# A mixture-of-experts stage rewritten as one program: deeper lag of the down products, splits on VectorE, routing weights through DRAM

## The chip, the cores and the metric

The kernel runs on one core of a Trainium2 chip. The metric is the device time in microseconds (us) of one execution. Three runs of the kernel before gave 3318.07, 3337.93 and 3340.95 us, median 3337.93. One more execution was profiled: 3319.7 us, of which 3317.8 us is the span from the first to the last instruction.

## The reference, cut to what matters

Two batches of 2048 tokens with 256 channels pass through a modulated attention layer and then through a modulated block of a second attention and a mixture of experts. All of it is float32. The change is about the last part:

```python
x = x + _attention(_rmsnorm(x, w_ln1), Wq, Wkva, Wkvb, Wo)     # only the product with Wo is in the changed stage
xn = _rmsnorm(x, w_ln2)
shared = jnp.mean(_experts(xf, sWg, sWu, sWd), axis=1)          # one shared expert
probs = jax.nn.softmax(xf @ Wgate + expert_bias, axis=-1)
topk_p, topk_i = jax.lax.top_k(probs, K)                        # K = 2 of E = 8
comb = jnp.sum(jax.nn.one_hot(topk_i, E) * (topk_p / jnp.sum(topk_p))[..., None], axis=1)
routed = jnp.einsum('ne,nec->nc', comb, _experts(xf, Wg, Wu, Wd))
out = residual + (shared + routed)
# _experts: g = silu(x @ Wg); u = x @ Wu; (g * u) @ Wd, per expert with I = 128 inner columns
```

The experts are computed densely: every token goes through all nine, and the routing weight of an expert, zero for most tokens, multiplies its inner activations.

## The kernel before, in words

The kernel is a row of stages, each in a `Block` with a barrier at its ends: modulation, first projections, first attention, second projections, second attention (`attention2`), and the experts' stage (`experts`, L1438). Matrix products are done three times on numbers split in two parts (`product3`, L127: low by high, high by low, high by high), so every operand exists as a rounded `_hi` and a rest `_lo = x - _hi`.

`experts` consists of three blocks, one after the other:

- `fold_weights` (L1396): GpSimd clears a tile, SyncE loads pieces of `Wkvb` and `Wo` and two constants, TensorE multiplies four pairs, ScalarE and VectorE split the products.
- `split_weights` (L134): ScalarE makes the high half of the experts' weights (L154), VectorE the low half (L160).
- the main block. Tokens are worked in eight blocks of 512 (four per batch; the two batches alternate). A token block has a *front* and nine *units*, one for each expert, the shared one last.

The front, by the step letters of the code: P splits the attention's output (load of 1 MB at L1545, high half on ScalarE L1593, low half on GpSimd L1571), A multiplies it by `Wo` (48 matmuls of 256 columns) and VectorE adds the residual; N and R are the norm (squares L1597, square root L1601); X transposes (L1765) and splits; L makes the logits (24 matmuls of 8 columns) and VectorE picks the two best; W takes the sigmoid of their difference; C transposes the weights.

A unit of expert j: G and U are the gate and up products (6 matmuls of 512 columns each) into the two halves of one of two PSUM pairs `pPair`; B (L1791) is one more matmul that spreads the routing weights of expert j over the 128 partitions; ScalarE takes the silu (L1616); VectorE multiplies it by the spread weights (L1718) and by the up product (L1726); ScalarE (L1620) and VectorE (L1642) split the result into `p_hi` and `p_lo`; D is the down product (12 matmuls of 256 columns), accumulated over the nine units in `pD`. After the last D, Y adds the residual on VectorE (L1734), and GpSimd multiplies by the modulation (L1574) and adds `x1` (L1578), before SyncE stores.

The order is written by hand and every engine runs through it (`order`, L1508). For each j it is G, B, U, then D of unit j-1, then a piece of the front of the *next* token block:

```python
after = {0: "P", 2: "A", 3: "NR", 4: "X", 5: "L", 6: "W", 7: "C"}
```

SyncE's own order (L1540 to L1557) for each block is: load of the attention's output for the next front, load of its residuals (one after the wait at L1551 for the output of the block before), then the wait for this block's result (L1555) and its store. The staging tiles of these loads and of the results lie in the memory of the unsplit weights (L1468, L1469).

Of the kernel before, what the change touches and what calls it, by code (L numbers as in the profile page):

```python
# [36 lines left out]

def modulation(nc, d, m):

    with ExitStack() as ctx:  # L40
        sb = lambda n, s, t=FP32: ctx.enter_context(nc.sbuf_tensor(n, s, t))
        sem = lambda n: nc.alloc_semaphore(n)
        cT, cE = sb("cT", [P, KT, B]), sb("cE", [P, KT, B])
# [11 lines left out]
        def _(sp):  # L55
# [4 lines left out]
            sp.dma_start(m.halves[:, :, :, :], d["halves"]).then_inc(loaded, 16)  # L60
# [31 lines left out]
        def _(dve):  # L92
# [11 lines left out]
            dve.tensor_copy(m.eye_half[:, :, :], m.halves[:, 0])  # L104
            dve.tensor_copy(m.after_half[:, :, :], m.halves[:, 1])
# [610 lines left out]
def attention2(nc, d, m):  # L716

    with ExitStack() as ctx:
# [35 lines left out]
        FILLS = 3  # L754
# [157 lines left out]
        def _(sp):  # L912
# [14 lines left out]
            for item in program:  # L927
# [23 lines left out]
        def _(pool):  # L951
            fills = [key1[b][ROWS:ROWS + 1].bitcast(FP32) for b in range(B)] + [ones[:, :]]
            for n, place in enumerate(fills):
                if n:
                    pool.wait_ge(filled, n)
                pool.memset(place, 1.0).then_inc(filled, 1)
# [481 lines left out]
def experts(nc, d, m):  # L1438

    with ExitStack() as ctx:  # L1442
        sb = lambda n, s, t=FP32: ctx.enter_context(nc.sbuf_tensor("e_" + n, s, t))
        sem = lambda n: nc.alloc_semaphore("e_" + n)
        sems = lambda n: [sem(f"{n}{b}") for b in range(2)]
        G, EX = HEADS // HG, E + 1
        wo_hi, wo_lo = sb("wo_hi", [P, G, C], F32R), sb("wo_lo", [P, G, C], F32R)
        wg_hi, wg_lo = sb("wg_hi", [P, KT, EX, I], F32R), sb("wg_lo", [P, KT, EX, I], F32R)
        wu_hi, wu_lo = sb("wu_hi", [P, KT, EX, I], F32R), sb("wu_lo", [P, KT, EX, I], F32R)
        wd_hi, wd_lo = sb("wd_hi", [P, EX, C], F32R), sb("wd_lo", [P, EX, C], F32R)  # L1450
        gate_hi, gate_lo = sb("gate_hi", [P, KT, E], F32R), sb("gate_lo", [P, KT, E], F32R)
        sel_st = sb("sel_st", [64, E, P])
        sel = sb("sel", [64, E, P], F32R)
        rank = sb("rank", [P, E])
        with ExitStack() as inner:
            st = lambda n, s, t=FP32: inner.enter_context(nc.sbuf_tensor("e_" + n, s, t))
            wo, kvb = st("wo", [P, G, C]), st("kvb", [P, G, P])
            fold_weights(nc, "e_fold", d, kvb,
                         [(wo[32 * j:32 * j + 32, :, :], d["Wo"].rearrange("(g j n) c -> j n g c", j=HG, n=HD2)[j, 0:32])
                          for j in range(HG)] + [(sel_st[:, :, :], d["sel"].rearrange("k (e p) -> k e p", e=E)),  # L1460
                                                 (rank[:, :], d["rank"].rearrange("(a n) -> a n", a=1).broadcast_to([P, E]))],
                         [(kvb[:, g, :], wo[:, g, :], wo_hi[:, g, :], wo_lo[:, g, :]) for g in range(G)])
        split_weights(nc, "e_w", [([], m.wg[:, :, :, :], wg_hi[:, :, :, :], wg_lo[:, :, :, :]),
                                  ([], m.wu[:, :, :, :], wu_hi[:, :, :, :], wu_lo[:, :, :, :]),
                                  ([], m.wd[:, :, :], wd_hi[:, :, :], wd_lo[:, :, :]),
                                  ([], m.gate[:, :, :], gate_hi[:, :, :], gate_lo[:, :, :])])

        o_st = m.wg[:, :, :, :].rearrange("p k e i -> p (k e i)")[:, 0:G * GT].rearrange("p (g t) -> p g t", g=G)  # L1468
        y = m.wu[:, :, :, :].rearrange("p k e i -> p (k e i)")[:, 0:B * NTILE * C].rearrange("p (b t c) -> p b t c", b=B, t=NTILE)  # L1469
        o_hi, o_lo = sb("o_hi", [P, G, GT], F32R), sb("o_lo", [P, G, GT], F32R)  # L1470
        xin, x1, x2 = sb("xin", [P, B, NTILE, C]), sb("x1", [P, B, NTILE, C]), sb("x2", [P, B, NTILE, C])
        xn, squares = sb("xn", [P, NTILE, C]), sb("squares", [P, NTILE, C])
        ssq, rms, rrms = sb("ssq", [P, NTILE]), sb("rms", [P, NTILE]), sb("rrms", [P, NTILE])
        xT_hi, xT_lo = sb("xT_hi", [P, B, KT, GT], F32R), sb("xT_lo", [P, B, KT, GT], F32R)
# [3 lines left out]
        comb = sb("comb", [P, NTILE, E])  # L1478
        combT = sb("combT", [64, B, GT], F32R)
# [4 lines left out]
        pB = ctx.enter_context(nc.psum_tensor("e_pB", [P, GT], FP32))  # L1484
        pG = ctx.enter_context(nc.psum_tensor("e_pG", [P, GT], FP32))

        filled, sel_ready, sp_passed = sem("filled"), sem("sel_ready"), sem("sp_passed")
        o_loaded, x_loaded, out_stored = sem("o_loaded"), sems("x_loaded"), sems("out_stored")
        x1_loaded, gate_psum = sems("x1_loaded"), sem("gate_psum")
        o_hi_ready, o_lo_ready = sem("o_hi_ready"), sem("o_lo_ready")  # L1490
        pair_psum, pair_read = sem("pair_psum"), sem("pair_read")
        x2_ready, ssq_ready, ms_ready, rms_ready, xn_ready = sem("x2_ready"), sem("ssq_ready"), sem("ms_ready"), sem("rms_ready"), sem("xn_ready")
        xT_hi_ready, xT_ready = sem("xT_hi_ready"), sem("xT_ready")
        g_psum, g_read, chain = sem("g_psum"), sem("g_read"), sem("chain")
        gap_ready, weight_ready, comb_ready, combT_hi_ready, combT_ready = (
            sem("gap_ready"), sem("weight_ready"), sem("comb_ready"), sem("combT_hi_ready"), sem("combT_ready"))
        b_psum, b_read = sem("b_psum"), sem("b_read")
        silu_ready, prod_ready, p_hi_ready, p_lo_ready = sem("silu_ready"), sem("prod_ready"), sem("p_hi_ready"), sem("p_lo_ready")
        down_done, y_sum, y_scaled, y_ready = sem("down_done"), sem("y_sum"), sem("y_scaled"), sem("y_ready")
        block = ctx.enter_context(nc.Block())  # L1500
        RING = 2

        FRONT = ("P", "A", "N", "R", "X", "L", "W", "C")

        def order(experts_too, front):  # L1508
            after = {0: "P", 2: "A", 3: "NR", 4: "X", 5: "L", 6: "W", 7: "C"}
            if not experts_too:  # L1510
                return [(s, 0) for s in FRONT]
            items = []
            for j in range(EX):
                items.append(("G", j))
                if j < E:
                    items.append(("B", j))
                items.append(("U", j))
                if j:
                    items.append(("D", j - 1))
                if front:  # L1520
                    items += [(s, 0) for s in after.get(j, "")]
            return items + [("D", E), ("Y", 0)]

        PAIRS = EX + 2

        def run(eng, work):

            work(order(False, True), -1, 1, 0, 0, 0, 0)
            for i in range(NGRP - 1):
                for b in range(B):  # L1530
                    work(order(True, True), i, b, i + b, 1 - b, 2 + PAIRS * (2 * i + b), b)
# [365 lines left out]
```

## Time and profile before

| What | us |
|---|---|
| Median of three runs | 3337.93 |
| Profiled execution, its own time | 3319.7 |
| Its span | 3317.8 |
| First instruction of the experts' stage (GpSimd's clearing, L1406) | 2727.9 |
| Start of the first load of the main block | 2751.1 |
| Start of the first unit's matmuls | 2791.5 |
| End of the last down product | 3307.5 |

The experts' stage is the last 590 us of the span. Everything before 2727.9 us is other stages, which the change touches in the second attention's list of loads and in one GpSimd fill alone. In the 40 slices of the page one slice is 82.9 us, so the stage is the last seven and a bit.

### The profile page before, as it was taken

What the parts mean: (1) busy time and instruction counts of PE and PEld (TensorE: products, weight loads), DVE (VectorE), ACT (ScalarE), POOL (GpSimd) and SP (SyncE); (2) the same over time, 40 slices, a digit from 0 to 9 for tenths busy, and PEclk for the clock granted to TensorE, in tenths of its full rate; (3) what the DMA queues carried; (4) which work ended last, traced back from release to release, by engine and by line L of the source; (5) the groups of instructions that cost most, each with busy time, mean ns of one, the idle gap of its engine ahead of it and who ended that gap; (6) DMA issues with size and microseconds to landing.
All of it is one profiled execution on the core that took longest, in us unless ns stands there. A gap on an engine that the chain in (4) does not pass through costs nothing. (4 is left out here: it accounts for less than half of the span.)

```text
span 3317.8 us, 47823 instructions
## 1 busy us (share of the span) xinstructions
PE 2852.9 (86%) x18768; PEld 1797.9 (54%) x18768; DVE 2049.9 (62%) x3301; ACT 1543.2 (47%) x3161; POOL 1312.8 (40%) x402
## 2 busy tenths in 40 slices
PE   3659999999999457668999999999999965888888
PEld 2534444444444145545566666666666634666666
DVE  4647888788885156647676776767676503444444
ACT  1225777677777222214455555555555533332232
POOL 3410000000000054525879788887979771111111
PEclk8967999899999578878999999999999977999889
DMA  3660331233300356571151321213131001101100
GB/s 94 202 124 5 44 45 19 31 44 46 39 10 8 101 166 183 188 184 30 23 129 42 68 49 45 54 37 68 23 68 42 11 17 51 32 32 61 35 32 13
DMA packets 153665, 207.01 MB, mean 62 GB/s; under 512 B 47840, under 2 KB 88928, under 8 KB 150304
## 3 DMA queue, kind: packets, MB, share of 16 engines
q1 hardware_dynamic: 152336, 198.58, 25.5%
q10 hardware_dynamic: 1104, 5.38, 0.5%
q8 instruction: 148, 2.42, 0.3%
q14 instruction: 77, 0.63, 0.1%
HBM read 121.59 MB, written 81.79 MB: 61 GB/s over the span
## 5 line engine op out<-in xcount | busy, mean ns | idle before, releaser
L990 ACT ACTIVATE a_prob<-a_pS 128x512 f32<-128x512 f32 (+3 forms) x1280 | 630.4, 534 | 594.8 <-PE a_pS L1072 269.2
L971 POOL TENSOR_TENSOR a_zsum<-a_zsum,a_prob 128x2048 f32<-128x2048 f32 (+1 forms) x200 | 882.0, 4410 | 50.9 <-ACT a_prob L990 24.2
L629 DVE TENSOR_REDUCE a_rowmax<-a_pR 128x2 f32<-128x1024 f32 (+3 forms) x640 | 651.7, 1061 | 144.1 <-PE a_pR L668 90.8
L610 ACT ACTIVATE a_prob<-a_pS 128x512 f32<-128x512 f32 (+3 forms) x1280 | 591.6, 539 | 287.6 <-PE a_pS L690 183.3
L1009 DVE TENSOR_REDUCE a_rowmax<-a_pR 128x2 f32<-128x1024 f32 x384 | 462.3, 1223 | 133.0 <-PE a_pR L1054 129.3
L1071 PE MATMUL a_pS<-a_q,a_key 128*128 128x512 f32 (+3 forms) x1280 | 507.9, 397 | 30.1 <-ACT a_prob L990 24.1
L1072 PE MATMUL a_pS<-a_q,a_key 65*128 65x512 f32 (+3 forms) x1280 | 474.7, 371 | 0.0
L1054 PE MATMUL a_pR<-a_key,a_q 128*128 128x512 f32 (+3 forms) x1280 | 395.8, 392 | 34.7 <-DMA a_q<-mid_q 22.4
L690 PE MATMUL a_pS<-a_q,a_key 49*128 49x512 f32 (+3 forms) x1280 | 406.7, 452 | 21.0 <-DMA a_q<-a_neg 15.7
L668 PE MATMUL a_pR<-a_key,a_q 48*128 48x512 f32 (+3 forms) x1280 | 330.3, 453 | 22.5 <-DMA a_q<-mid_qk 16.3
L1071 PEld LDWEIGHTS a_pS<-a_q,a_key 128*128 128x128 f32 x1280 | 247.8, 194 | 161.2 <-ACT a_prob L990 72.4
L706 PE MATMUL a_pO<-a_prob,a_val 128*32 128x512 f32 (+3 forms) x2560 | 317.0, 569 | 0.2
L1012 DVE CUSTOM_DVE_ANT_0 a_pR<-a_pR,causal 128x384 f32<-128x384 f32 (+3 forms) x512 | 240.5, 513 | 105.0 <-PE a_pR L1054 103.2
L690 PEld LDWEIGHTS a_pS<-a_q,a_key 49*128 49x128 f32 x1280 | 193.4, 197 | 185.6 <-ACT a_prob L610 115.3
L595 POOL COPY a_val<-v 128x256 f32<-128x256 f32 x32 | 11.4, 400 | 713.1 <-PE a_pO L706 698.6
L1054 PEld LDWEIGHTS a_pR<-a_key,a_q 128*128 128x128 f32 x1280 | 227.9, 198 | 86.3 <-issue 32.1
L1084 PE MATMUL a_pO<-a_prob,lat 128*32 128x512 f32 (+3 forms) x2560 | 262.5, 536 | 0.4 <-ACT a_prob L990 0.4
L1072 PEld LDWEIGHTS a_pS<-a_q,a_key 65*128 65x128 f32 x1280 | 246.2, 192 | 28.9
L668 PEld LDWEIGHTS a_pR<-a_key,a_q 48*128 48x128 f32 x1280 | 157.5, 198 | 163.1 <-DVE a_rowmax L629 96.1
L1026 DVE RECIPROCAL a_pR<-a_pR 128x512 f32<-128x512 f32 x32 | 107.7, 3366 | 129.7 <-PE a_pR L1095 129.7
L969 POOL TENSOR_TENSOR a_zsum<-a_prob 128x2048 f32<-128x2048 f32 x24 | 110.3, 4596 | 178.7 <-ACT a_prob L990 178.7
L1574 POOL TENSOR_TENSOR wu<-wu,mod 128x1024 f32<-128x1024 f32 x8 | 19.1, 2389 | 386.9 <-DVE wu L1734 386.9
(237 smaller groups left out, 4094.1 us busy)
## 6 DMA issues: line engine op xcount, KB each, us to landing
a_q<-mid_q SPq DMA_DIRECT2D x192, 256.0 KB, 6.4
a_key<-mid_qk SPq DMA_DIRECT2D x42, 256.0 KB, 9.0
a_q<-mid_qk SPq DMA_DIRECT2D x42, 256.0 KB, 15.8
mid_qk<-p_qk_hi SPq DMA_DIRECT2D x32, 256.0 KB, 2.8
mid_qk<-p_qk_lo SPq DMA_DIRECT2D x32, 256.0 KB, 3.3
mid_q<-p_n_hi SPq DMA_DIRECT2D x32, 256.0 KB, 3.0
mid_q<-p_n_lo SPq DMA_DIRECT2D x32, 256.0 KB, 3.3
mid_q<-p_r_hi SPq DMA_DIRECT2D x32, 256.0 KB, 2.4
```

The costliest lines, as they stand in the source:

```text
L610: act.activation(prob[:, n % 4, h, at:GT], pS[:, (HG * n + h) % NS, at:GT], ACT.Exp).then_inc(exp_ready, 1)
L629: dve.tensor_reduce(rowmax[:, c % 2, :, j, t, kc], pR[:, bank, :, 0:n], axis=AX.X, op=ALU.max).then_inc(r_read, 1)
L668: mm = pe.matmul(pR[:, bank, half, 0:n], q[g % 2][rows48, j, at:at + P], key[g % 2][rows48, j, GT * kc:GT * kc + n], start=True, stop=kc < c)
L690: mm = pe.matmul(pS[:, n % NS, at:GT], key[g % 2][rows49, h // 2, P * kt:P * kt + P], q[g % 2][rows49, h // 2, c * GT + at:(c + 1) * GT], ...
L706: mm = pe.matmul(pO[32 * h:32 * h + 32, at:GT], val[g % 2][:, kt, h, :], prob[:, n % 4, h, at:GT], start=(kt == 0), stop=kt == 4 * c + 3)
L971: pool.tensor_tensor(zsum[:, ring, :, at:GT], zsum[:, ring, :, at:GT], prob[:, step % 4, :, at:GT], ALU.add).then_inc(z_added, 1)
L990: act.activation(prob[:, n % 4, h, at:GT], pS[:, (HG * n + h) % NS, at:GT], ACT.Exp, scale=SCALE).then_inc(exp_ready, 1)
L1009: dve.tensor_reduce(rowmax[:, c % 2, 2 * j:2 * j + 2, t, kc], pR[:, bank, :, :], axis=AX.X, op=ALU.max).then_inc(r_read, 1)
L1054: mm = pe.matmul(pR[:, bank, half, 0:n], q0[:, c, 2 * j + half, P * t:P * t + P], key0[b][:, GT * kc:GT * kc + n], start=True, stop=True)
L1071: pe.matmul(pS[:, n % NS, at:GT], key0[b][:, keys], q0[:, c, h, at:GT], start=True, stop=False)
L1072: mm = pe.matmul(pS[:, n % NS, at:GT], key1[b][0:ROWS + 1, keys], q1[0:ROWS + 1, c, h, at:GT], start=False, stop=not diagonal)
L1084: mm = pe.matmul(pO[32 * h:32 * h + 32, at:GT], m.lat[:, b * (T // P) + kt, :], prob[:, n % 4, h, at:GT], start=(kt == 0), stop=kt == 4 * ...
```

## The change

- The three blocks of the experts' stage become one: the folding and the weight splits are steps of one program, between the steps of the first front. Their loads (`e_kvb`, `wo`, `rank`) move into the second attention's list of loads, nine more DMAs there, behind a wait for four GpSimd fills.
- The program runs over all 72 units (0 to 8 of each token block, the shared expert now first), batch by batch. D of a unit stands behind the products of the unit after the next. The front of the next block is spread one step per unit, A behind unit 0 of a block, and the split of the attention's output ("O") behind unit 8, two blocks ahead. Its load is issued at step X.
- The matmul B and its operands are gone. The routing weights, transposed, are stored to DRAM (16 KB) and loaded back by one source row for all 128 partitions: 6 experts (1536 KB) at once after the store, 2 (512 KB) later. The silu is multiplied by that tile.
- GpSimd does nothing in the stage. The low half of the attention's output and both operations of Y are on VectorE, Y in three parts behind units 1, 2 and 3 of the next block.

```diff
 def attention2(nc, d, m):
                     load_keys(sp, 1, slice(0, T), key_loaded[1])
+                    sp.wait_ge(filled, FILLS)
                     for src, place in m.expert_loads:
                         sp.dma_start(place, src).then_inc(experts_loaded, 16)
...
+            m.expert_loads = [(heads_kvb[j], m.e_kvb[32 * j:32 * j + 32, :, 32 * j:32 * j + 32]) for j in range(HG)]
+            m.expert_loads += [(heads_wo[j, 0:32], m.wo[32 * j:32 * j + 32, :, :]) for j in range(HG)]
+            m.expert_loads += [(d["rank"].rearrange("(a n) -> a n", a=1).broadcast_to([P, E]), m.rank[:, :])]
 def experts(nc, d, m):
-            fold_weights(nc, "e_fold", d, kvb,
...
-        split_weights(nc, "e_w", [([], m.wg[:, :, :, :], wg_hi[:, :, :, :], wg_lo[:, :, :, :]),
...
-        def order(experts_too, front):
-            after = {0: "P", 2: "A", 3: "NR", 4: "X", 5: "L", 6: "W", 7: "C"}
...
+        def order():
+            items = [("fold", 0), ("O", 0), ("split", 0), ("split", 1), ("A", 0), ("N", 0), ("split", 2), ("R", 0), ("X", 0),
+                     ("split", 3), ("L", 0), ("K", 0), ("O", 1), ("W", 0), ("C", 0)]
+            for n in range(BLOCKS):
+                front = {0: [("A", n + 1)], 1: [("N", n + 1)], 2: [("R", n + 1)], 3: [("X", n + 1)], 4: [("L", n + 1)],
+                         5: [("K", n + 1)], 6: [("W", n + 1)], 7: [("C", n + 1)], 8: [("O", n + 2)]}
+                for j in range(UNITS):
+                    k = UNITS * n + j
+                    items.append(("U", k))
+                    items += [x for x in front[j] if x[1] < BLOCKS]
+                    if k >= 2:
+                        items.append(("D", k - 2))
+                    if n and j < 4:
+                        items += [("Y", n - 1, j - 1)] if j else []
+            last = UNITS * BLOCKS
+            return items + [("P", last), ("D", last - 2), ("D", last - 1)] + [("Y", BLOCKS - 1, part) for part in range(3)]
 # SyncE
+            def load_spread(n, part):
+                experts_in = slice(0, EARLY) if part == 0 else slice(EARLY, E)          # EARLY = 6
+                if n:
+                    sp.wait_ge(prod_ready, UNITS * (n - 1) + experts_in.stop + 1)
+                sp.dma_start(spread[:, experts_in], d["comb"][n, experts_in].rearrange("(a e) t -> a e t", a=1)
+                             .broadcast_to([P, experts_in.stop - experts_in.start, GT])).then_inc(spread_loaded[part], 16)
...
+                if step == "C":
+                    s = n % 2
+                    sp.wait_ge(combT_ready, n + 1)
+                    sp.dma_start(d["comb"][n], combT[:, s, :]).then_inc(comb_stored[s], 16)
+                    sp.wait_ge(comb_stored[s], 16 * (n // 2 + 1))
+                    load_spread(n, 0)
+                if step == "U" and n % UNITS == 1:
+                    load_spread(n // UNITS, 1)
+                if step == "X" and n + 1 < BLOCKS:
+                    load_o(n + 1)                    # waits for the matmuls of A of block n
 # ScalarE, step U
+                    act.activation(silu[:, n % 2, :], pPair[:, pairs["U", n] % 2, 0, :], ACT.Silu).then_inc(silu_ready, 1)
+                if step in "UP" and n:
+                    high_half(n - 1)
 # VectorE
+                if step == "O":
+                    dve.wait_ge(o_hi_ready, n + 1)
+                    dve.tensor_tensor(o_lo[:, :, :], o_lo[:, :, :].bitcast(FP32), o_hi[:, :, :], ALU.subtract).then_inc(o_lo_ready, 1)
...
+                if step == "U":
+                    dve.wait_ge(silu_ready, n + 1)
+                    if j:
+                        dve.tensor_tensor(prod[:, s, :], silu[:, s, :], spread[:, j - 1, :], ALU.mult).then_inc(prod_begun, 1)
+                    if n:
+                        low_half(n - 1)
+                    dve.wait_ge(pair_psum, use + 1)
+                    dve.tensor_tensor(prod[:, s, :], pPair[:, use % 2, 1, :], (prod if j else silu)[:, s, :], ALU.mult).then_inc(prod_ready, 1)
...
+                    if part == 1:
+                        dve.tensor_tensor(y, y, m.mod[:, n // NGRP, 5, :].unsqueeze(1).broadcast_to([P, NTILE, C]), ALU.mult).then_inc(y_scaled, 1)
+                    if part == 2:
+                        dve.wait_ge(x1_loaded, 16 * (n + 1))
+                        dve.tensor_tensor(y, y, x1[:, :, :], ALU.add).then_inc(y_ready, 1)
 # TensorE
-                    if step == "B":
-                        pe.matmul(pB[:, :], sel[:, j, :], combT[:, b, :], start=True, stop=True).then_inc(b_psum, 1)
+                    if use >= 2:
+                        pe.wait_ge(pair_read, use - 1)     # of steps U, A and X
+                if step == "L":
+                    if n == 0:
+                        pe.wait_ge(split_lo, len(splits))
+                if step == "D":
+                    if j == 0 and at:
+                        pe.wait_ge(y_sum, at)
+                    pe.wait_ge(p_lo_ready, n + 1)
```

## Rows read from the trace of the kernel before

**Rows 1.** The page: the span.
```profile
span 3317.8 us, 47823 instructions
```

**Rows 2.** Windows: length; busy us (instructions) of PE, PEld, DVE, ACT, POOL; PEclk; DMA.
```profile
2727.90:2751.10 23.20, 3.90 (x8) 2.17 (x8) 9.28 (x8) 7.79 (x8) 0.53 (x1) 0.57 0.16 38
...
2751.10:2791.50 40.40, 15.90 (x85) 15.01 (x86) 7.02 (x26) 8.91 (x16) 5.44 (x2) 0.58 0.31 104
...
2791.50:2851.30 59.80, 56.72 (x316) 44.87 (x314) 28.80 (x55) 23.52 (x38) 4.62 (x1) 0.98 0.00 1
...
2919.20:2988.10 68.90, 58.27 (x309) 46.41 (x308) 29.20 (x54) 21.64 (x36) 9.33 (x3) 0.90 0.12 39
...
3055.90:3126.70 70.80, 61.29 (x310) 48.92 (x309) 29.30 (x54) 21.63 (x36) 9.35 (x4) 0.86 0.12 38
...
3264.60:3307.50 42.90, 41.97 (x219) 32.87 (x218) 19.03 (x26) 11.03 (x18) 4.77 (x2) 1.00 0.04 13
...
3307.50:3317.80 10.30, 0.04 (x1) 0.00 (x0) 1.22 (x1) 0.00 (x0) 4.67 (x2) 0.60 0.15 51
```

**Rows 3.** Timeline of TensorE, third block: start, us, what [idle before, releaser].
```profile
2935.33 0.79 PE L1791 MATMUL e_pB<-e_combT,e_sel 64*128 64x512 f32 x1 [7.47 <-DVE e_prod L1718]
```

**Rows 4.** Timeline of ScalarE, same stretch.
```profile
2932.16 1.91 ACT L1593 ACTIVATE e_o_hi<-wg 128x2048 fp32r<-128x2048 f32 x1 [9.39 <-DMA wg<-mid_o]
```

**Rows 5.** Chain of work that ended last, same stretch: start, us, what.
```profile
2924.68 7.46 DMA wg<-mid_o
```

**Rows 6.** Windows of TensorE's two clock levels; columns as in Rows 2.
```profile
2930.80:2941.00 10.20, 5.37 (x15) 3.83 (x16) 5.20 (x5) 3.92 (x5) 4.53 (x1) 0.50 0.23 74
...
3104.90:3111.60 6.70, 6.70 (x17) 4.74 (x18) 3.72 (x16) 0.60 (x1) 0.00 (x0) 0.50 0.00 0
...
3217.50:3307.00 89.50, 85.44 (x479) 68.47 (x479) 41.57 (x75) 27.93 (x48) 4.79 (x2) 1.00 0.02 7
```

**Rows 7.** Timeline of TensorE, fifth block: the first matmul of L.
```profile
3102.60 0.17 PE L129 MATMUL e_pG<-e_gate_hi,e_xT_lo 128*128 128x8 f32 x1
```

**Rows 8.** Timeline of TensorE, last block: L129 opens each group of matmuls.
```profile
3295.83 0.39 PE L129 MATMUL e_pPair<-e_xT_hi,e_wg_lo 128*128 128x512 f32 x1
...
3299.24 0.28 PE L129 MATMUL e_pD<-e_wd_hi,e_p_lo 128*128 128x256 f32 x1
...
3300.66 0.39 PE L129 MATMUL e_pPair<-e_xT_hi,e_wg_lo 128*128 128x512 f32 x1
...
3303.41 0.29 PE L129 MATMUL e_pD<-e_wd_hi,e_p_lo 128*128 128x256 f32 x1
```

**Rows 9.** Windows of one tile, TensorE: e_wo_hi (A), e_xn (X), e_pG (L, C).
```profile
3217.50:3264.60 47.10, 5.92 (x32) 1.00 0.01 1
...
3217.50:3264.60 47.10, 1.04 (x8) 1.00 0.01 1
...
3217.50:3264.60 47.10, 3.33 (x28) 1.00 0.01 1
```

**Rows 10.** Groups by line from 2650 us: busy, mean ns, idle before, releasers.
```profile
L1571 POOL TENSOR_TENSOR e_o_lo<-wg,e_o_hi 128x2048 fp32r<-128x2048 f32 x8 | 36.3, 4538 | 99.5 <-ACT e_o_hi L1593 99.5
...
L154 ACT ACTIVATE e_wu_hi<-wu 128x2304 fp32r<-128x2304 f32 x1 | 2.1, 2106 | 0.0
...
L160 DVE TENSOR_TENSOR e_wg_lo<-wg,e_wg_hi 128x2304 fp32r<-128x2304 f32 x1 | 2.6, 2557 | 2.5 <-ACT e_wg_hi L154 2.5
```

**Rows 11.** Timeline of VectorE, third block.
```profile
2936.70 2.53 DVE L1642 TENSOR_TENSOR e_p_lo<-e_prod,e_p_hi 128x512 fp32r<-128x512 f32 x1 [0.70 <-ACT e_p_hi L1620]
```

**Rows 12.** DMA issues: KB each, median us to landing.
```profile
mid_o<-a_out SPq DMA_DIRECT2D x32, 128.0 KB, 2.0
...
wmod<-in_wmod_dram SPq DMA_DIRECT2D x1, 1536.0 KB, 6.3
```

**Rows 13.** Chain of waits, first front: ScalarE's table load before the square root.
```profile
2773.76 1.28 ACT L1601
```

**Rows 14.** Timeline of SyncE's queue, folding: four DMA issues.
```profile
2730.29 1.86 SPq L1415 DMA_DIRECT2D e_wo<-in_Wo_dram  x4
```

More of the change, by code:

```diff
@@ L1451, in experts @@
[L1451 to L1457, printed above, removed]
-            fold_weights(nc, "e_fold", d, kvb,
[L1459 to L1462, printed above, removed]
@@ L1524, in experts @@
[L1524 to L1531, printed above, removed]
-            i = NGRP - 1
-            work(order(True, True), i, 0, i, 1, 2 + PAIRS * 2 * i, 0)
-            work(order(True, False), i, 1, 0, 0, 2 + PAIRS * (2 * i + 1), 1)
-        tok = lambda name, b, i: d[name].rearrange("b (i t p) c -> b i p t c", t=NTILE, p=P)[b, bass.ds(i, 1)].rearrange("a p t c -> (a p) t c")
+        splits = [(m.wg[:, :, :, :], wg_hi[:, :, :, :], wg_lo[:, :, :, :]), (m.gate[:, :, :], gate_hi[:, :, :], gate_lo[:, :, :]),
+                  (m.wu[:, :, :, :], wu_hi[:, :, :, :], wu_lo[:, :, :, :]), (m.wd[:, :, :], wd_hi[:, :, :], wd_lo[:, :, :])]
@@ new lines, in _ @@
+            load_o(0)
+            load_xin(0)
+            load_xin(1)
+            load_x1(0)
+            for step, n, *rest in program:
+                if step == "C":
[8 more added lines that the diff above has]
+                    load_o(n + 1)
+                if step == "L" and n + 1 < BLOCKS and n:
+                    load_xin(n + 1)
+                if step == "Y" and rest[0] == 2:
+                    sp.wait_ge(y_ready, n + 1)
+                    sp.dma_start(token_block(d, "out", *divmod(n, NGRP)), x2[:, n % SLOTS]).then_inc(out_stored[n % SLOTS], 16)
+                    if n + 1 < BLOCKS:
+                        load_x1(n + 1)
@@ new lines, in _, with link, low_half @@
+            per_token = lambda t: t.unsqueeze(2).broadcast_to([P, NTILE, E])
+            ranks = m.rank[:, :].unsqueeze(1).broadcast_to([P, NTILE, E])
+            links = 0
+            def link(ins):
+                nonlocal links
+                links += 1
+                ins.then_inc(chain, 1)
+                dve.wait_ge(chain, links)
+            def low_half(k):
+                dve.wait_ge(p_hi_ready, k + 1)
+                dve.tensor_tensor(p_lo[:, k % 2, :], prod[:, k % 2, :], p_hi[:, k % 2, :], ALU.subtract).then_inc(p_lo_ready, 1)
@@ L1802, in _ @@
-            run(pe, work)
+                if step == "D":
+                    at, j = divmod(n, UNITS)
+                    if j == 0 and at:
+                        pe.wait_ge(y_sum, at)
+                    pe.wait_ge(p_lo_ready, n + 1)
+                    for t in range(NTILE):
+                        tokens = slice(P * t, P * t + P)
+                        mm = product3(pe, pD[:, t, :], p_hi[:, n % 2, tokens], p_lo[:, n % 2, tokens], wd_hi[:, expert(j), :], wd_lo[:, expert(j), :],
+                                      j == 0 and t % 2 == 0, j == UNITS - 1, skip_group_check=True)
+                    mm.then_inc(down_done, 1)
```

513 lines of the change are left out of this document (223 added, 290 removed).

## The prediction

> **What bounds the kernel now.** I started at the page, for the span [rows 1], and cut the experts' stage into stretches by the windows view [rows 2]. It takes 590 us: 23.2 us for folding and splitting, 40.4 us for the first front, then eight token blocks, and 10.3 us behind the last down product. A middle block takes 68.9 us with TensorE busy for 58.3; VectorE (29.2), ScalarE (21.6) and GpSimd (9.3) are not near it. So TensorE's queue sets the time, and three things make a block longer than its products need.
>
> - It waits. 68.9 - 58.3 = 10.6 us of the block it is idle, 7.47 of them in one gap [rows 3]. There ScalarE, in order, stands for 9.39 us in front of the split of the attention's output, for a load [rows 4]. The chain of waits says why the load is late: its 7.46 us begin only after SyncE's queue has stored the block before, for which it waits on GpSimd's last addition (L1578) [rows 5].
> - Its clock falls. Behind such a gap it is granted half of full speed (1.2 instead of 2.4 GHz) for 10.2 us [rows 6]. Over the block the share is 0.90, so 0.10 x 68.9 x 2 = 13.8 us at half speed and 6.9 us lost.
> - Products that the change drops: B, eight times per block.
>
> The last block has no front and runs nearly without gaps: 42.9 us at a clock of 1.00, 42.0 busy [rows 2]. It shows what units cost when nothing is late.
>
> **One unit after the change.** In that block a unit with B repeats after 3300.66 - 3295.83 = 4.83 us; in the shared unit, which has no B, gate and up take 3303.41 - 3300.66 = 2.75 us; a down product takes 3300.66 - 3299.24 = 1.42 us [rows 8]. A unit without B is 2.75 + 1.42 = 4.17 us. The bound above is that removing B saves only its own time of some 0.4 us (4.83 - 4.17 is 0.66): 0.24 x 64 = 15 us more. I take 4.17, as the row is that very sequence.
>
> **The front on TensorE.** A 5.92, X 1.04, L and C 3.33 us busy [rows 9], 10.3 in sum. Modelled ends overlap the next matmul by 0.16 to 0.2 us, once per piece, so 9.6.
>
> **Blocks.** 72 x 4.17 + 7 x 9.6 = 300.2 + 67.2 = 367.4 us, if nothing is late. Is something late? I follow each queue, from TensorE's first matmul of a unit as zero.
>
> - *Unit.* Gate ends at 1.4; silu to 2.0; VectorE's product with the spread tile to 2.7, the low half of the unit before to 3.4, the product with up to 4.1 (instructions of 512 columns take some 0.7, 19.03 / 26 [rows 2]). The pair must be free at 8.3 (two units) and the low half is wanted at 6.9, since D lags by two units. Now D stands one unit behind and waits. Moving it costs nothing.
> - *O behind unit 8.* ScalarE 2.7 to 4.6; VectorE, 2048 columns by the row of 2304 [rows 10], 2.27 us, to 6.9. A behind the next unit 0 starts at 4.17 + 2.75 = 6.9. No slack: the cover is the down product and the unit's products, and each 1 us beyond costs 1 us.
> - *X, L, K, W, Y on VectorE.* Its work per block becomes 29.2 + 2.3 + 2 x 1.22 = 33.9 of 47.1 us. The first part of Y (1.22 us [rows 2]) has the 2.75 us of unit 2 as cover before D of the next block needs `pD`. GpSimd's own instructions go, and with them what VectorE loses beside them: a low half of 2.53 us next to GpSimd's subtraction [rows 11] instead of 0.7.
> - *ScalarE* keeps its table loads and stays at 22 us.
> - *The routing weights.* From C to the silu of unit 1 of the next block TensorE has 2 D, unit 8, unit 0, A, D and a gate product: 3 x 1.42 + 2 x 2.75 + 5.8 + 1.4 + silu 0.6 = 17.5 us. Against it: copy 0.6, store of 16 KB 2.0 (nearest row 128 KB), load of 1536 KB 6.3 (a load from as many different rows) [rows 12], 8.9 in sum. Hidden with 8.6 us over, and 4 more before TensorE runs dry. In the first block the cover is some 12 us, still enough. The 512 KB behind it are due five units later. SyncE waits for the store before it loads, with nothing urgent behind it.
> - *Loads of the attention's output* are issued at X, four units ahead: the 7.47 us gap goes.
>
> A rule of the Trainium skill speaks against that load (DMA: Bandwidth & Descriptors, Latency and other measured facts): copies whose 128 rows lay megabytes apart by a power of two ran at 103 instead of 207 GB/s, put down to all streams meeting one memory channel. One row read by all 128 would be that case. By it the load takes 15.3 us and the sum grows by 2 to 3 us in the first block alone.
>
> **Clock.** With the gaps gone their falls should go too. But one fall has no gap in front: at 3104.9 TensorE is busy for all of 6.7 us at half speed, just behind the start of L's matmuls of 8 columns at 3102.60 [rows 6, 7]. The two blocks with a share of 0.86 (one in [rows 2]) have such a fall, the other five have not. L stays. I take two falls again, 2 x 6.7 / 2 = 6.7 us, bounds 0 and seven (23.5). The first unit starts after idling: in the first block now 0.02 x 59.8 us of share are missing [rows 2], +1.2. For small waits 0.3 per front, +2.1.
>
> The skill's page TensorE: Matmul & The Clock Gate (HAM oscillation) lets the clock fall for an idle engine only. By it there are no such falls and the sum is 6.7 us lower; the row contradicts it.
>
> **Prologue.** Now the 23.2 us pass before the load of the first front, then 40.4 us to the first unit [rows 2]. After, the load starts at +0.6 and the fold lies beside it (5 us of load; four small products 4 us). On the path: 0.6 + 40.4, less GpSimd's 4.54 for VectorE's 2.27 = -2.3; the third split before R, 2.11 + 2.56 less the 1.28 us table load that it hides [rows 13], +3.4; the fourth before L, its ScalarE half beside VectorE's work on X, +3.3; O of block 1 before W, +2.3 [rows 10]. Sum 47.7 instead of 63.6 us: 15.9 saved, first unit at 2775.6. Bounds: all splits hidden (38.7) and none of ScalarE's (54).
>
> **Second attention.** Nine more DMA issues at one place; at 1.86 / 4 = 0.47 us each [rows 14] they hold SyncE's queue for 4.2 us. TensorE has work from other loads there; I take 0, bounds 0 and 4.2.
>
> **Tail.** 10.3 us now, with VectorE 1.22 and GpSimd 4.67 [rows 2]; three VectorE parts 3.66 instead of 5.89: 8.1.
>
> **Sum.** 2775.6 + 367.4 + 6.7 + 1.2 + 2.1 + 8.1 = 3161.1 us of span, and 1.9 around it (3319.7 against 3317.8): 3163 against 3319.7, 157 us less. The profiled run lies 18 us under the median of the three runs, which spread over 23 us; so from 3337.9: **3181 us**. By its own bounds this case reaches from 3163 to 3205.
>
> **Rivals.**
>
> *The clock does not hold.* If blocks still miss a tenth, each loses 6.9 us as now: 48 instead of 6.7, 3222 us. For it: falls without a gap. Against: 89.5 us at 1.00 in the densest stretch, with one L in it [rows 6]. Chance 0.15.
>
> *VectorE's order becomes the wait.* It does nearly everything in line and waits for ScalarE and TensorE between. If TensorE keeps the 10.6 - 7.5 = 3.1 us of other idle time per block, at A for O or at D for Y, and each costs 5.1 us of clock: 7 x 8.2 = 57, 3238 us. Against: the slack of the units. Chance 0.13.
>
> *The load is no earlier in effect*, since SyncE holds it behind stores and loads of the routing weights. Gap and clock stay, 7 x 12.6 = 88: 3269 us. Against: what stands before it is due earlier. Chance 0.03.
>
> *The broadcast load is slow* (the side on which it is slower than before). The tile is single; its load cannot start before C and unit 6's product, so a block repeats in no less than load time + 2.6 + 30 us. Up to 19 us nothing happens. From 34 us on (five times the 6.3) it is as slow as before; at 45 us a block takes 78, 8 x 30 = 241 more: 3422 us. For it: no row shows a load of this size from one row. Against: the row of a plain load. Chance 0.05. The skill's rule above is a mild form of it and changes nothing but the first block.
>
> Better than my case, with no falls and splits hidden: 0.06. My case: 0.58.
>
> **Numbers.** 3181 us. Under 3150 lies 0.06, over 3245 the last two rivals and part of the third, so 3150 to 3245 holds a good 8 in 10. What can be told from no change is about 1%, 33 us. Faster by more: all but part of the slow load, 0.93; within 1% 0.02; slower 0.05.
>
> **What would show it.** First unit near 2776; windows of 47 us per block with TensorE over 95% busy and a clock of 0.97 or more; no gap over 1 us at A; VectorE never waiting for the tile of routing weights from the second block on; that load landing in 6 to 9 us. I am wrong if VectorE's product waits for the load, if the clock's share stays at 0.9 with TensorE busy, or if A waits for the low half.

## The result, and the profile after

| | before | after |
|---|---|---|
| Median of 4 runs each, us | 3332.82 | 3157.15 (3152.57 to 3171.17) |
| Ratio | | 0.9485, 95% interval 0.9438 to 0.9532 |
| Span of the profiled run | 3317.8 | 3150.7 |
| Experts' stage | 589.9 | 428.4 |
| of it until the first gate product | 63.2 | 46.8 |
| from the first gate product to the last down product | 516.4 | 373.8 |
| behind it | 10.3 | 7.9 |

The kernel is 5.1% faster. The prediction was 3181 us, 3150 to 3245. The time lies in that range, and the mechanism of the main case came true. But it lies 6 us under the 3163 to 3205 that the prediction gave as this case's own bounds; the point on the sum, below, says which term did that. (The 63.6 us of the prediction until the first unit are 63.2 by the first gate product itself, at 2791.17.)

The page, the span, against [rows 1]:
```profile
span 3150.7 us, 47527 instructions
```
Windows of the changed kernel, columns as in [rows 2]: prologue, a middle block, a block just behind a clock fall, the whole stretch of the units, the tail.
```profile
2722.30:2769.07 46.77, 20.09 (x93) 17.93 (x93) 20.33 (x33) 16.82 (x21) 0.00 (x0) 0.57 0.24 79
2821.10:2868.70 47.60, 47.60 (x303) 42.51 (x302) 29.28 (x56) 20.86 (x36) 0.00 (x0) 1.00 0.30 100
2894.36:2943.25 48.89, 48.89 (x307) 43.53 (x307) 29.27 (x56) 20.86 (x36) 0.00 (x0) 1.00 0.28 96
2769.07:3142.80 373.73, 373.65 (x2318) 332.77 (x2316) 219.46 (x417) 156.22 (x271) 0.00 (x0) 0.99 0.27 91
3142.80:3150.70 7.90, 0.03 (x1) 0.00 (x0) 3.67 (x3) 0.00 (x0) 0.00 (x0) 0.76 0.20 66
```
A middle block takes 47.6 us instead of 68.9, and TensorE is busy for all of it, at full clock. Over 373.7 us it is idle for 0.1.

What TensorE waits for in the stage (us in total, times, longest of one; in front of the arrow what waits, behind it what ended the wait). All five stand before the first unit:
```profile
PE e_pPair L1746 <- DVE e_xn L1653: 9.4, 1, 9.4
PE e_pPair L1725 <- PEq L1839: 7.6, 1, 7.6
PE e_pG L129 <- DVE e_wd_lo L1634: 6.0, 1, 6.0
PE e_pPair L129 <- DVE e_o_lo L1637: 5.7, 1, 5.7
PE e_pG L1765 <- DVE e_comb L1687: 5.7, 1, 5.7
```
The gap of [rows 3] and ScalarE's wait of [rows 4] have no counterpart: ScalarE's main wait is now for TensorE.

Timeline of VectorE where a block ends, then of TensorE; against the prediction's "no slack" at O:
```profile
2862.78 2.29 DVE L1637 TENSOR_TENSOR e_o_lo<-e_o_lo,e_o_hi 128x2048 fp32r<-128x2048 f32 x1 [0.43 <-ACT e_o_hi L1578]
```
```profile
2865.22 0.36 PE L129 MATMUL e_pPair<-e_wo_hi,e_o_lo 128*128 128x256 f32 x1
```
The low half ends at 2865.07, A begins at 2865.22: 0.15 us to spare.

DMA issues of the page, against [rows 12]:
```profile
e_spread<-mid_comb SPq DMA_DIRECT2D x8, 1536.0 KB, 6.3
```
One source row per expert, read for all 128 partitions, lands in 6.3 us, as fast as the load of this size from different rows.

The one clock fall among the units; timeline of TensorE at the end of an L, and the window of the fall:
```profile
2888.66 0.17 PE L129 MATMUL e_pG<-e_gate_hi,e_xT_lo 128*128 128x8 f32 x1
...
2890.81 0.25 PE L131 MATMUL e_pG<-e_gate_hi,e_xT_hi 128*128 128x8 f32 x1
2890.92 0.34 PE L129 MATMUL e_pG<-e_gate_hi,e_xT_lo 128*128 128x8 f32 x1
```
```profile
2890.95:2894.36 3.41, 3.41 (x17) 3.41 (x18) 1.33 (x7) 0.00 (x0) 0.00 (x0) 0.50 0.91 262
```
There is no gap in front of it, and the small matmuls of L stretch from 0.25 to 0.34 us. The fall costs half its 3.41 us.

**Where 142.6 us of the units' stretch went.** I split the stretch of each run into three parts. The first is TensorE's idle time. The second is half of what it was busy at half clock (lost clock). The rest is its products at full clock, with what small waits take from their overlap. All come from its matmuls and the clock changes in the trace.

| run | stretch | idle | lost clock | products |
|---|---|---|---|---|
| before | 516.4 | 63.5 | 33.5 | 419.3 |
| after | 373.8 | 0.1 | 2.9 | 370.8 |
| after, second profile | 376.9 | 0.1 | 6.1 | 370.7 |
| e1_early_load | 454.4 | 21.2 | 11.8 | 421.4 |
| e2_lag_two | 501.8 | 62.5 | 24.9 | 414.4 |
| e3_early_and_lag | 433.1 | 11.3 | 4.9 | 416.9 |
| a1_lag_one | 432.0 | 43.6 | 4.4 | 384.0 |
| a2_dummy_b | 411.9 | 0.1 | 7.4 | 404.5 |
| a3_late_tile | 410.2 | 17.8 | 19.3 | 373.1 |
| a4_later_tile | 453.3 | 49.7 | 33.5 | 370.1 |
| a5_y_gpsimd | 405.1 | 17.3 | 16.4 | 371.3 |
| a6_o_gpsimd | 399.0 | 13.1 | 15.2 | 370.7 |
| a7_prologue | 379.2 | 0.1 | 8.8 | 370.3 |
| a8_spread_l | 374.5 | 0.1 | 1.3 | 373.1 |

Of the 142.6 us, 63.4 were idle time, 30.6 lost clock and 48.5 products.

**Where the clock falls.** In these profiles every fall that begins among the units begins at one of two places. One is a wait of TensorE of 1.8 us or more (all shorter ones are under 1 us): during it, or up to 1.5 us behind its end. The other is the lot of 24 small matmuls of L: 2.1 to 4.1 us behind its first matmul. Counted are the waits, and those with a fall; the lots (seven in each run, a8 has none in one piece), and those with a fall; and the clock lost at each.

| run | waits of 1.8 us or more, each | with a fall | lost there | lots of L with a fall | lost there |
|---|---|---|---|---|---|
| before | 7 of 1.8, 6 of 6.2 to 7.5 | 11 of 13 | 25.1 | 2 | 6.8 |
| e1_early_load | 7 of 1.8 | 3 of 7 | 5.1 | 2 | 5.1 |
| e2_lag_two | 6 of 8.1 to 8.9 | 6 of 6 | 16.5 | 4 | 6.8 |
| e3_early_and_lag | none | | | 2 | 3.4 |
| after / its second profile | none | | | 1 / 2 | 1.7 / 5.1 |
| a1_lag_one | 7 of 2.6 | 2 of 7 | 3.2 | 0 | 0 |
| a2_dummy_b | none | | | 3 | 5.1 |
| a3_late_tile | 7 of 1.8 to 2.2, 1 of 3.0 | 3 of 8 | 5.1 | 6 | 11.9 |
| a4_later_tile | 8 of 5.9 to 6.5 | 8 of 8 | 20.4 | 7 | 11.9 |
| a5_y_gpsimd | 6 of 2.8 | 6 of 6 | 10.0 | 3 | 5.1 |
| a6_o_gpsimd | 6 of 2.2 | 1 of 6 | 1.7 | 6 | 11.9 |
| a7_prologue | none | | | 3 | 6.8 |

What is missing to the lost clock above is the slow start of the first unit (1.0 to 2.3 us). In all, 41 of 91 lots have a fall.

### The profile page after: what moved, and what is told of

Same layout as the page of the kernel before. It is cut to its first block and busy times, and to the rows that moved or that the text cites. A ratio compares the mean times of both kernels' runs of the same rounds, so it can differ in the third digit from the quotient of the medians.

```text
span 3150.7 us, 47527 instructions
## 1 busy us (share of the span) xinstructions
PE 2765.7 (88%) x18704; PEld 1769.9 (56%) x18704; DVE 2053.7 (65%) x3314; ACT 1534.5 (49%) x3157; POOL 1237.4 (39%) x377
## 5 line engine op out<-in xcount | busy, mean ns | idle before, releaser
L672 PE MATMUL a_pR<-a_key,a_q 48*128 48x512 f32 (+3 forms) x1280 | 330.3, 453 | 22.8 <-DMA a_q<-mid_qk 16.6
L1089 PEld LDWEIGHTS a_pO<-a_prob,lat 128*32 128x32 f32 x2560 | 71.6, 109 | 123.3 <-issue 88.2
```

The costliest lines, as they stand in the source:

```text
L672: mm = pe.matmul(pR[:, bank, half, 0:n], q[g % 2][rows48, j, at:at + P], key[g % 2][rows48, j, GT * kc:GT * kc + n], start=True, stop=kc < c)
L1089: mm = pe.matmul(pO[32 * h:32 * h + 32, at:GT], m.lat[:, b * (T // P) + kt, :], prob[:, n % 4, h, at:GT], start=(kt == 0), stop=kt == 4 * ...
```

## Experiments

Ratios are to the kernel before on the same chip, with 95% intervals.

**From the kernel before: one part alone.**

*e1_early_load.*
```diff
 SyncE: load of the attention's output for the next front
-    behind the wait for this block's result, the store, and the residuals' wait
+    ahead of them; the rest of the order as it is
```


> The kernel before with one thing changed: SyncE issues the load of the next attention output ahead of the wait for the block's result, so it has landed when ScalarE comes to it. Theory (the gap and what the clock does behind it are worth what the trace shows): the 7.2 us gap and 10.2 us at half clock (5.1 us lost) go in seven blocks: 7 x 12.3 = 86 us less, ratio 0.974, stage (first instruction to end) 504 instead of 590 us. Rival (another wait takes its place, since ScalarE, GpSimd and VectorE still have the same work in line): only the gap or less, under 50 us, ratio 0.985 or above.

Measured: 0.979 (0.974 to 0.985), stretch -62.0. Between the theory and its rival. The theory had read two sizes wrongly. The kernel before has this wait in six blocks, not seven:
```profile
PE e_pB L1791 <- DVE e_prod L1718: 41.2, 6, 7.5
```
And of the 58.0 us of falls behind these six gaps TensorE is busy for 33.3 only, so 16.6 us are lost, not 7 x 5.1. The theory should have said 41.2 + 16.6 = 57.8 us, which fits the 62.0. Waits of TensorE for the low half in e1, from 2770 us on:
```profile
PE e_pD L129 <- DVE e_p_lo L1649: 20.6, 22, 1.8
```
The 7.5 us gap is gone with 42.3 us of idle time and 21.7 of lost clock. What stays is the down product one unit behind, beside GpSimd's long subtraction.

*e2_lag_two.*
```diff
-                    items.append(("D", j - 1))
+                    items.append(("D", j - 2))       # and ("D", E - 1), ("D", E) at the end of a block
```


> The kernel before with the down products two units behind instead of one, nothing else. Theory: the waits of down products for the low half (1.8 + 0.3 + 0.7 us per block) and one fall of the clock (3.4 us, 1.7 lost) go: 7 x 4.5 = 31 us less, ratio 0.991. Rival (the late load sets the block, and what is gained before it is waited for there): about nothing, ratio 0.997 to 1.0.

Measured: 0.995 (0.992 to 0.998), stretch -14.6, half of what the theory said.
```profile
PE e_pB L1791 <- DVE e_prod L1718: 51.2, 6, 8.9
PE e_pPair L1765 <- DVE e_xn L1661: 10.2, 8, 6.0
PE e_pPair L129 <- DVEq L1728: 6.1, 7, 0.9
```
(The 6.0 us at X are the first front's.) The waits of D are gone, but the big gap grew from 7.5 to up to 8.9 us: TensorE only comes sooner to the product that stands for the load. Idle time fell by 1.0 us in all.

*e3_early_and_lag*: both edits.

> Both at once on the kernel before. Theory (TensorE's queue is then dense at full clock, and the two add): 86 + 31 = 117 us less, ratio 0.965, stage 473 us; what is left to the changed kernel's 428 is the matmul B (64 x 0.66 = 42) and the prologue (16). Rival (not additive: one cures the other's wait): 86 us, ratio 0.974.

Measured: 0.977 (0.973 to 0.982), stretch -83.3, 7 more than the two alone (76.6). The lag is worth 21.3 us once the load is early. In total time it comes no lower than its rival's figure, and the medians of e1 and e3 lie 5.7 us apart where the stretches differ by 21.3. In e3's profile the experts' stage begins 16 us later; such differences come between profiles of one code too (below), so the total time can't settle it. Against the changed kernel 59.3 us are left, 46.1 of them products.

**From the changed kernel: one part taken back.**

*a1_lag_one.*
```diff
-                    if k >= 2:
-                        items.append(("D", k - 2))
+                    if k >= 1:
+                        items.append(("D", k - 1))
```


> The changed kernel with the down products one unit behind. Theory: VectorE makes the low half only behind the product with the tile of the next unit, 3.5 us after the unit's first matmul, the down product is due at 2.75: TensorE waits 0.75 us in each of 72 units, 54 us more, stage 482 instead of 428, ratio 0.965. Rival (the lag is not needed, VectorE has slack): under 10 us more, ratio 0.95.

Measured: 0.971 (0.966 to 0.977), stretch +58.2. Waits of TensorE in the stage:
```profile
PE e_pD L129 <- DVE e_p_lo L1625: 25.4, 45, 0.7
PE e_pD L129 <- DVE e_x L1711: 18.2, 7, 2.6
```
The size is the theory's, a part of its content is not: 18.2 us are Y's first addition, which frees `pD` and with a lag of one has no unit to hide behind. Another 13.2 us are no gaps at all but products that lose their overlap behind 45 short waits (384.0 against 370.8). Nothing of it is clock (+1.5).

*a2_dummy_b*: adds, in 56 units, a matmul of B's shape that nobody reads.
```diff
+                        if half == 0 and j < 7:
+                            if j == 0:
+                                pe.wait_ge(combT_ready, at + 1)
+                            pe.matmul(pG[:, 1, :], wg_hi[0:64, 0, 0, :], xT_hi[0:64, at % 2, 0, :], start=True, stop=True)
```


> The changed kernel with one more matmul of B's shape (64 rows, 512 columns) between the gate and the up product in units 0 to 6 of each block, 56 in all; nobody reads its result. Theory (removing B saves the difference of a unit with and without it, 4.83 - 4.17): 56 x 0.66 = 37 us more, stage 465. Rival (only its own 0.42 us): 23.5 us more, stage 452.

Measured: 0.964 (0.959 to 0.969), stretch +38.1, of which products +33.7: 33.7 / 56 = **0.60 us** each, though the matmul itself is shown with less:
```profile
L1779 PE MATMUL e_pG<-e_xT_hi,e_wg_hi 64*128 64x512 f32 x56 | 28.4, 507 | 0.0
```
So leaving out B is worth 0.60 a unit, 38.5 us in 64 units, near the 0.66 of [rows 8] and not the 0.42 of the bound. The other 10 of 48.5 us of products have no shown cause. Some may be of the kind that a1 shows, overlap lost behind short waits; but e3, whose down products hardly wait for the low half any more (0.7 us in all), still has 7.6 of them (416.9 - 370.8 - 38.5).

*a3_late_tile* and *a4_later_tile*: the tile of routing weights is loaded later, behind A in unit 0 and behind unit 1's products.
```diff
-                    load_spread(n, 0)                # at step C
+                if step == "U" and n % UNITS == 0:   # a4: == 1
+                    sp.wait_ge(pair_psum, ...)       # a3: the matmuls of A of the next block; a4: those of unit 1
+                    load_spread(n // UNITS, 0)
```


> The changed kernel with the load of the routing weights (1536 KB) issued only behind A, some 3.4 us before VectorE wants it; it lands 3.1 us late. Theory (TensorE has 4 us more before it runs dry; only the first part of Y, queued behind on VectorE, is 1.5 us late for the next block's first down product): 7 x 1.5 = 10 us more. Rival A (each us that VectorE waits is a us of time): 8 x 3.1 = 25 us more. Rival B (hidden): 0.

> The same load issued behind the products of unit 1, 2.8 us later still. Theory: the first part of Y is 5.7 us late, TensorE stands for that long in seven blocks, and its clock falls behind it as it did behind the 7 us gap (3.4 to 5.1 us lost): 7 x 9.1 to 10.8 = 64 to 75 us more, clock share of the stage 0.9. Rival (the gap alone, since it is shorter and the clock holds): 40 us more, share 0.98.

Measured: a3 0.962 (0.952 to 0.973), stretch +36.4; a4 0.975 (0.972 to 0.979), +79.5. Waits of VectorE and TensorE in a3:
```profile
DVE e_prod L1697 <- DMA e_spread<-mid_comb: 47.3, 8, 6.2
```
```profile
PE e_pD L129 <- DVE e_x L1713: 14.5, 7, 2.2
PE e_pD L129 <- DVE e_p_lo L1627: 3.0, 1, 3.0
```
VectorE stands some 6 us in each block and TensorE only about 2: the cushion of the lag is there, and what breaks through is again Y's first addition, but for the first block's 3.0 us. I had expected the tile 3.1 us late and Y 1.5; it is 5.9 and 2.1. The price is double TensorE's idle time, since 16.4 us of clock come with it. Timeline of TensorE and window of the fall behind a gap, second block:
```profile
2835.66 0.38 PE L129 MATMUL e_pD<-e_wd_hi,e_p_lo 128*128 128x256 f32 x1 [1.91 <-DVE e_x L1713]
```
```profile
2837.15:2840.56 3.41, 3.41 (x10) 2.69 (x9) 2.88 (x8) 2.06 (x4) 0.00 (x0) 0.50 0.00 0
```
Only three of the eight gaps have such a fall. The other six falls, with 11.9 us of the clock lost, come 12 to 15 us behind the gap, at L. First matmul of L in the fourth block, and the window of the fall:
```profile
2949.70 0.17 PE L129 MATMUL e_pG<-e_gate_hi,e_xT_lo 128*128 128x8 f32 x1
```
```profile
2953.20:2956.61 3.41, 3.41 (x13) 2.93 (x12) 0.70 (x4) 0.00 (x0) 0.00 (x0) 0.50 0.81 257
```
The late tile brings them (six of seven lots here, one or two of seven in the changed kernel). How a gap that is over by then does it stays open, and in a1 gaps of 2.6 us brought none at L.

+17.7 idle, +16.4 lost clock, +2.3 products. I had reckoned 10 us, without clock. In a4, with gaps up to 6.5 us, it is +49.6 and +30.6, in sum a little over the theory's 64 to 75 us; there all eight gaps and all seven lots have a fall, and its rival failed. Even so a4 is faster than the kernel before.

*a5_y_gpsimd* and *a6_o_gpsimd*: Y's multiplication and last addition, or O's low half, back on GpSimd.
```diff
-        dve.tensor_tensor(y, y, m.mod[...], ALU.mult)       # and the addition of x1; a6: o_lo = o_lo - o_hi
+        pool.tensor_tensor(y, y, m.mod[...], ALU.mult)      # likewise, same waits and semaphores
```


> The changed kernel with the multiplication and the last addition of Y back on GpSimd. Theory (off the path but for the tail): 2.3 us more. Rival (VectorE's instructions with two operands in SBUF are held up beside GpSimd's, 2.5 us instead of 0.7 as in the kernel before, and A or D then waits): 10 us or more.

> The changed kernel with the low half of the attention's output back on GpSimd. Theory (no slack there: VectorE's ends 0.15 us before A starts; GpSimd takes 4.54 instead of 2.29 us): 2.1 us of wait in seven blocks and 2.3 in the prologue, 17 us more; with VectorE held up beside it up to 30. Rival (hidden behind the products): 2.3 us more.

Measured: a5 0.966 (0.957 to 0.974), stretch +31.3; a6 0.957 (0.951 to 0.963), +25.2. Timelines of GpSimd, VectorE and TensorE in a5:
```profile
2843.55 2.41 POOL L1619 TENSOR_TENSOR e_x<-e_x,mod 128x1024 f32<-128x1024 f32 x1 [119.61 <-DVE e_x L1725]
2846.04 2.73 POOL L1623 TENSOR_TENSOR e_x<-e_x 128x1024 f32<-128x1024 f32 x1
```
```profile
2844.27 2.24 DVE L1709 TENSOR_TENSOR e_prod<-e_silu,e_spread 128x512 f32<-128x512 f32 x1 [0.80 <-ACT e_silu L1607]
2846.44 2.89 DVE L1639 TENSOR_TENSOR e_p_lo<-e_prod,e_p_hi 128x512 fp32r<-128x512 f32 x1
...
2850.73 1.14 DVE L1667 TENSOR_SCALAR e_xn<-e_x,e_rrms 128x256 f32<-128x256 f32 x4
```
```profile
2852.02 0.52 PE L1753 MATMUL e_pPair<-eye,e_xn 128*128 128x128 f32 x3 [2.84 <-DVE e_xn L1667]
```
The rival was right. VectorE is relieved of 2.44 us and loses more: two instructions of 0.69 us take 2.24 and 2.89 while GpSimd works, each ending some 0.55 us behind GpSimd's. The norm starts 8.48 us behind Y's first addition (2842.25) instead of 4.72, X comes 2.84 us late in six blocks, 17.0 us, and the clock adds 13.5, 10.0 of it at these waits. The tail is 2.3 us longer, as the theory had it. In a6 A waits for the slower low half, 2.2 us in six blocks, 13.0 us, and the clock adds 12.3: a fall at one wait of six, the rest at L. The 2.3 us more in the prologue did not come (46.4 us for 46.8).

**The changed kernel, improved.**

*a7_prologue.*
```diff
-            items = [..., ("split", 1), ("A", 0), ("N", 0), ("split", 2), ("R", 0), ("X", 0),
-                     ("split", 3), ("L", 0), ("K", 0), ("O", 1), ("W", 0), ("C", 0)]
+            items = [..., ("split", 1), ("split", 2), ("split", 3), ("A", 0), ("N", 0), ("R", 0), ("X", 0),
+                     ("O", 1), ("L", 0), ("K", 0), ("W", 0), ("C", 0)]
```


> The changed kernel with all four weight splits before A of the first front and the split of block 1's attention output before its logits, so that they run while TensorE does A and L. Theory: 3.4 + 3.3 + 2.3 = 9.0 us less on the way to the first unit, 38.1 instead of 47.1 us, ratio to the kernel before 0.946. Rival (VectorE is still splitting when A ends, or squares wait on ScalarE): 3 us or less.

Measured: 0.951 (0.946 to 0.956). The first unit comes 38.6 us behind the fold's first matmul instead of 46.8, as expected; but the units of this profile have three clock falls, 13.7 us together, where the first profile of the changed kernel has one of 3.4 us: +5.4. (The expectation of a8 counts four, with the slow start of the first unit.) The total time doesn't show the gain.

*a8_spread_l*: a7, and L in four lots.
```diff
+                        if half == 0 and j == 4 and at + 1 < BLOCKS:   # behind the gate half of unit 4
+                            route(at + 1, 0)                           # 6 of the 24 matmuls
...                                                                     # lot 1 behind U, 2 within the down product, 3 behind it
```


> The changed kernel with two edits: the prologue of the run a7 (all four splits before the first attention product, the second o load's halves before the routing's) and the 24 routing logit products of a block laid in four lots of 6: behind the gate half of U in the fifth unit, behind U, in the middle of the down product and behind it, in place of one lot of 24. Work is the same. Theory: TensorE's clock falls within the stage begin in the lot of 24 (after: one, 2.9 us lost; a7: four, 6 us lost); with the lot broken up, none is left, the first-G-to-last-D loop takes 373.8 - 2.9 = 371 us, the prologue stays at 38 to 39 us against 46.8, and the stage is 11 us shorter than the changed kernel's: ratio to before 0.9485 - 0.0033 = 0.945, and 0.9965 of the changed kernel beside it. Rival: the falls come from the mean of what TensorE did before, not from that lot, and then they stay: loop 375 to 380 us with as many falls as in a7, ratio within 0.1% of a7's beside it. Second rival: the logits are done 1.4 us later and VectorE, which waits for them in its order, comes late for the next unit: TensorE idles about 1 us at the down product in each of 7 blocks, +7 us.

> The changed kernel itself once more, beside a8 on the same chip, so that a8's gain is read against it and not against the kernel before. Theory: 0.9485 of the kernel before within its interval, stage 425 to 435 us, loop 371 to 380 us by how many clock falls of some 3 us each it meets (one in the first profile). Rival: the first profile was a lucky one, and the loop has as many falls as a7's (four or more), 379 us or above.

Measured: a8 0.9485 (0.9447 to 0.9523), the changed kernel beside it 0.9512 (0.9476 to 0.9548), with a stage of 431.3 and a stretch of 376.9 us, as its theory had it. Windows of a8: prologue, units, tail.
```profile
2729.67:2766.99 37.32, 19.02 (x93) 16.89 (x93) 20.41 (x33) 16.84 (x21) 0.00 (x0) 0.59 0.29 99
2766.99:3141.45 374.46, 374.37 (x2318) 331.06 (x2316) 219.38 (x417) 156.30 (x271) 0.00 (x0) 1.00 0.27 91
3141.45:3149.30 7.85, 0.00 (x0) 0.00 (x0) 3.67 (x3) 0.00 (x0) 0.00 (x0) 0.73 0.19 67
```
In a8 the clock holds from 2769.61 to 3145.08. The two falls of the changed kernel's second profile:
```profile
2964.29:2971.12 6.83, 6.83 (x26) 6.15 (x26) 1.33 (x7) 0.47 (x1) 0.00 (x0) 0.50 0.59 181
3015.49:3018.91 3.42, 3.42 (x16) 3.32 (x16) 1.33 (x7) 0.00 (x0) 0.00 (x0) 0.50 0.90 276
```
Their L's begin at 2962.14 and 3012.87. In the four profiles without gaps (two of the changed kernel, a7, a2), nine falls come at the 28 lots of 24, each 2.2 to 4.1 us behind the lot's first matmul and nowhere else in blocks of some 48 to 53 us. That they come at L is shown by this. In a8 there is none in 7 blocks. If 9 in 28 were the plain chance, none in 7 would come one time in 15, so that breaking L up cures them is likely but not proven.

Cutting L up costs 2.5 us of products (373.1 against a mean of 370.6 in the changed kernel and a7), over half of the 4.6 us that the clock gives back (1.3 lost against a mean of 5.9). The gain of a8 is the prologue: the stage takes 419.6 us against 428.4 and 431.3. Mean of six runs each, 3156.2 against 3166.3 us: 10.2 less, 95% interval 0.4 to 20.0. That is the best version here, by 0.3%, just told apart from the changed kernel. Of its rivals, the second failed, as TensorE waits for nothing among a8's units; the first, that the falls don't hang on the lot, found no fall to rest on.

## Why the prediction was right, point by point

- **Bound and mechanism.** Idle time, lost clock, and B: all three went. The measured block of 47.6 us is 9 x 4.17 + 9.6 = 47.1 and 0.5 of small change. The present cost of the clock was misread, though. The prediction took half of all time at half clock, 6.9 us a block, for lost; but in 10.2 us of [rows 6] TensorE is busy for 5.37 only, and only busy time loses by the clock. The trace of before has 33.5 us of lost clock in all, 4.8 a block, and the big gap in six blocks, not seven. So the 5.1 us of clock a block in the second and third rival are too much (the gap and the clock behind it are 57.8 us in e1's terms, where the third has 88). The forecast does not use these terms: it is added up from products.
- **Unit.** Gate, up and down products repeat after 4.19 us for 4.17. B was the 0.66 step of [rows 8], 0.60 by a2; the 15 us bound was not needed.
- **The lag.** "Costs nothing" hid its worth: with D one behind, the new unit would lose 58 us. Tried alone in the old order it is 15. The text had named the low half as what waits; it gave Y's first addition the cover of unit 2 without saying that the lag of two is what gives it, and that is a third of the 58.
- **O behind unit 8.** Predicted to end as A begins; 0.15 us to spare. a6 shows the edge: a low half 2.2 us longer cost 2.2 us of wait a block, and nearly as much clock with it.
- **Routing weights.** Load 6.3 us as in the row, cover as reckoned: in the third block it lands 9.2 us before VectorE wants it, for 8.6 reckoned, and VectorE never waits for it. The Trainium skill (DMA: Bandwidth & Descriptors, Latency and other measured facts) has 103 GB/s for rows 4 or 8 MiB apart; that one row read 128 times would be such a case was my reading of it. By it the load would have taken 15.3 us, an estimate from that figure. The trace does not agree with the reading: this source shows the plain rate. The "4 more before TensorE runs dry" was right as well: in a3 VectorE stands 5.9 us and TensorE 2.1. What I left out was the clock, which nearly doubled the price there. The fourth rival's two limits for a slow load do not agree (19 us by the cover, 47.1 - 32.6 = 14.5 by its own formula for a block); no run has a load in between.
- **Clock.** Two falls taken; one and two found, of 3.41, 6.83 and 3.41 us, for 6.7 each. They lost 1.7 and 5.1 us, for 6.7. Whether a profile has one, two or three (a7) is chance: the count of two was a guess that held. All follow L without a gap, as the row of before had it. The Trainium skill's page TensorE: Matmul & The Clock Gate (HAM oscillation) ties a fall to an idle engine; the trace does not agree for those at L, and agrees for those at waits.
- **Prologue** 46.8 for 47.7; **tail** 7.9 for 8.1.
- **Second attention.** The stages before were 5.6 us shorter in this profile. Over all profiles, the experts' stage starts between 2719 and 2752 us with the new list of loads and between 2725 and 2744 with the old one, so the 0 to 4.2 us of the nine DMAs can't be read.
- **The sum.** 3163 us for the profiled run, measured 3152.6: 10.4 too high, of which the earlier stages are 5.6, the units 3.6, prologue and tail 1.1. The step that failed by most is the last one: I added 18.2 us because the profiled run of before lay so far under its median. After, this distance is 4.6. In the second set of the changed kernel the profiled run lies 16.4 us above its median. A distance from one profile to a median of three is scatter, not a property to carry over; that is the other 13.6 of the 24 us between 3181 and 3157, and it is why the time fell under the case's own bounds. Those bounds are loose themselves: the ones named term by term, all at once, give 3165 to 3223, and the text does not say how they became 3163 to 3205.

## What to carry to other kernels

Read the product time from the densest block of the profile. Count the clock's price beside idle time of TensorE, but from busy time at half clock and not from the granted share alone. It came near the idle time again in a3, a5 and a6 (gaps of 2 to 3 us), and was next to nothing in a1, with seven gaps of 2.6 us. A lag in a software pipeline is worth what stands between producer and consumer in the *new* order, every user of the accumulator included; tried alone in the old order it showed a quarter of it, since another wait took up the gain. And moving work off a busy VectorE to GpSimd can make VectorE later.

## What was not expected of the hardware

- A matmul of 64 rows by 512 columns between others of 128 rows costs 0.60 us of the row of products, while its record shows 0.51.
- 24 matmuls of 8 columns take 2.60 us in one lot; laid in four lots, a block takes 0.4 us more (2.5 / 7).
- VectorE's instructions of 0.69 us take 2.24 and 2.89 beside GpSimd's of 2.41 and 2.73 on 128 partitions of float32 in SBUF.
- Clock falls come without any gap, 2.2 to 4.1 us behind the first of L's 24 small matmuls: 9 times in 28 lots where TensorE has no gap, 6 or 7 times in 7 lots in a3, a4 and a6, whose blocks also have a gap of 2 to 6 us. Each lasts 3.41 or 6.83 us.
- A gap of 1.8 to 2.6 us is followed at once by a fall in some cases only (all of that size in the profiles here: 14 of 34), one of 2.8 us in six of six in a5.
